# Moving the table products of a two-layer expert kernel, splitting its weight chunks later, and giving its last steps an order of their own

## The reference

```python
# layer 0, weights of the sequence's expert: Wi 256x1024, Wo 1024x256
h = gelu(x @ Wi[e] + bi[e]);  r = h @ Wo[e] + bo[e] + x
x = layernorm(r, eps=1e-12) * gamma[e] + beta[e]
# layer 1: down 256->64, an expert matrix 64x64, up 64->256
a = gelu(x @ down_W.T + down_b)
o = a @ expert_W[d].T + expert_b[d] + domain_emb[d]
x = layernorm(o @ up_W.T + up_b + x, eps=1e-5) * ln_gamma + ln_beta
```

## Time and profile before

| | us |
|---|---|
| median of 3 runs | 488.36 (488.33 to 488.38) |
| profiled execution | 488.29, of which the span from first to last instruction is 486.5 |
| PE busy | 458.1 (94% of the span) |
| ACT busy | 362.3 (74%) |
| DVE busy | 341.8 (70%) |
| POOL busy | 343.7 (71%) |
| mean granted TensorE clock | 0.980 of full speed |
| chain that ended last | PE 89%, DVE 3%, issue 2%, POOL 2%, ACT 2% |

### The profile page before, as it was taken

How to read it: one execution, slowest core, us unless ns; L and a number is a source line. 1 busy time by engine, 2 the same in 40 slices (tenths; PEclk the granted TensorE clock), 3 DMA queues, 4 the chain that set the end, 5 groups by cost and what they waited for, 6 DMA issues and landing times.

```text
span 486.5 us, 18826 instructions
## 1 busy us (share of the span) xinstructions
PE 458.1 (94%) x5724; PEld 423.3 (87%) x5725; DVE 341.8 (70%) x910; ACT 362.3 (74%) x1087; POOL 343.7 (71%) x567
## 2 busy tenths in 40 slices
PE   3599999999999999999999999999999999999972
PEld 2388999999999999999999999999999999888861
DVE  7677777777777777777777787777777766665352
ACT  2499777887777877778877788777787777776631
POOL 5043677887778877887778877887778877754565
PEclk9889999999999999999999999999999999999995
DMA  3924334333333343433433333333332222220001
GB/s 105 333 73 106 95 99 104 104 102 92 98 100 95 103 104 87 99 96 102 104 89 95 102 101 98 86 98 101 101 98 65 60 62 61 62 56 25 26 22 34
DMA packets 66806, 44.33 MB, mean 91 GB/s; under 512 B 41537, under 2 KB 58322, under 8 KB 66642
## 3 DMA queue, kind: packets, MB, share of 16 engines
q1 hardware_dynamic: 65744, 43.68, 33.4%
q10 hardware_dynamic: 1026, 0.21, 0.2%
HBM read 35.47 MB, written 8.39 MB: 90 GB/s over the span
## 4 chain that ended last, share of the span: by engine, by line
PE 89%; DVE 3%; issue 2%; POOL 2%; ACT 2%; DMA 0%; POOLq 0%; DVEq 0%
PE p_o L1019 12%; PE p_o L1017 12%; PE p_o L1018 12%; PE p_h L1006 12%; PE p_h L1008 11%; PE p_h L1007 11%; PE p_d L1029 7%; PE p_u L1043 6%; PE p_t L1051 3%; PE p_u L1039 2%; PE p_o L1117 1%; PE p_h L947 1%; DVE W L810 1%; ACT h L639 0%; ACT ctab L591 0%
## 5 line engine op out<-in xcount | busy, mean ns | idle before, releaser
L1006 PE MATMUL p_h<-x_hi,W 128*128 128x128 f16 (+1 forms) x1088 | 183.5, 217 | 3.3 <-issue 3.3
L1007 PE MATMUL p_h<-x_lo,W 128*128 128x128 f16 (+1 forms) x1088 | 183.3, 217 | 0.0
L1008 PE MATMUL p_h<-x_hi,W 128*128 128x128 f16 (+1 forms) x1088 | 183.3, 217 | 0.0
L639 ACT ACTIVATE h<-p_h,bi_tile 128x128 f32<-128x128 f32 (+1 forms) x544 | 149.0, 359 | 0.0
L1018 PE MATMUL p_o<-W,h_hi 128*128 x512 | 139.6, 273 | 0.0
L1017 PE MATMUL p_o<-W,h_hi 128*128 x512 | 139.6, 273 | 0.0
L1019 PE MATMUL p_o<-W,h_lo 128*128 x512 | 139.5, 273 | 0.0
L1006 PEld LDWEIGHTS p_h<-x_hi,W 128*128 x1088 | 105.7, 98 | 9.3 <-issue 8.0
L1007 PEld LDWEIGHTS p_h<-x_lo,W 128*128 x1088 | 105.7, 98 | 1.9
L1008 PEld LDWEIGHTS p_h<-x_hi,W 128*128 x1088 | 105.6, 98 | 0.0
L539 POOL TENSOR_TENSOR rs<-mv,neg_half 128x1 f32<-128x1 f32 x64 | 55.1, 861 | 69.7 <-DVE mv L882 69.7
(11 more groups left out here) (167 smaller groups left out, 825.5 us busy)
## 6 DMA issues: line engine op xcount, KB each, us to landing
stage<-in_w SPq DMA_DIRECT2D x56, 256.0 KB, 2.7
x_nat<-in_x SPq DMA_DIRECT2D x128, 64.0 KB, 2.1
out<-y SPq DMA_DIRECT2D x128, 64.0 KB, 2.0
x_T<-in_xT SPq DMA_DIRECT2D x126, 64.0 KB, 2.2
W<-in_w SPq DMA_DIRECT2D x8, 256.0 KB, 4.8
g_t<-in_gamma SPq DMA_DIRECT2D x1, 1024.0 KB, 7.0
W<-in_expert_W SPq DMA_DIRECT2D x2, 128.0 KB, 3.0
upT<-in_up_W SPq DMA_DIRECT2D x2, 64.0 KB, 2.6
```

What stands on the lines that cost most here:

```text
L639: ins = nc.scalar.activation(h[:, c, mine], p_h[parity][:, c, mine], ACT.Gelu, bias=bi_tile[:, parity, n, c:c + 1], scale=1.0 / (XS * WS))
L1006: mm(out, hi, x_hi[:, parity, k, mine], start=(k == 0), stop=False)
L1007: mm(out, hi, x_lo[:, parity, k, mine], start=False, stop=False)
L1008: ins = mm(out, lo, x_hi[:, parity, k, mine], start=False, stop=(k == KD - 1))
```

## The change

Six things change.

- **Tables.** All four rounds move behind the first products, one in each of the steps 0 to 3 (`rounds`). Rounds 0 and 1 use `p_t` and `p_d`, rounds 2 and 3 `p_u` and `p_d` (`table_banks`). The matmuls for `u_s` now write `p_h1`. Round r waits for `c_copied` = 2r, `down` of step 3 for 6, `up` of step 4 for 8, round 3 for `a1_done`.
- **Chunks.** Steps 0 to 3 split one chunk each, steps 4 and 5 two each, later steps one as before.
- **First loads.** SP issues four of the first expert's chunks, then x of tile 1, then the other four.
- **Drain.** In steps 64 to 68 DVE has an order of its own, PE transposes behind the second products and not between them, and for tiles 60 to 63 gamma and beta are applied by DVE (`late_gamma`, `late_out`, semaphores `yl_done`, `y_late`), not by POOL.
- **Places.** The two further numbers of a mixed tile stand in the same row of `idx`, which is six wide now; steps 60 to 64 load six numbers at once.
- **Buffers.** The second half of the turned expert matrices lies in `ew[0]`, not in `yg`.

```diff
         def chunks(i, weights):
-            if isinstance(i, int) and i < EARLY:
-                return [(2 * i + q, (2 * i + q, 1, 2 * i + q)) for q in range(2)]
+            if isinstance(i, int) and i < LEAD - EARLY:
+                js = [i] if i < 4 else [2 * i - 4, 2 * i - 3]
+                return [(j, (j, 1, j % SLOTS_W)) for j in js]
             return [(i + EARLY, weights)] if weights else []
...
+        def rounds(i):
+            return [i] if isinstance(i, int) and i < 4 else []
+        def table_banks(r):
+            return [(p_t if r < 2 else p_u)[:, :], p_d[:, :]]
+        def drain(i):
+            return isinstance(i, int) and i >= TILES
+        def late(j):
+            return isinstance(j, int) and TILES - 4 <= j < TILES
...
-            for m in FIRST_ORDER:
-                sp.dma_start(first_stage[m], t["w"][bass.ds((expert + m) * P, P), :]).then_inc(first_in[m], 16)
+            load_first(FIRST_ORDER[:4])
             sp.wait_ge(idx_ready, SRC_READY)
             load_turned(indices(sp, IDX_SP + 6, 2, B - 1), 1, 1)
+            load_first(FIRST_ORDER[4:])
...
 ACT, before the steps
-            copy_round(0, both)
             for n, m in enumerate(FIRST_ORDER):
                 if n == 2:
                     high_x(0, 0)
+                if n == 4:
+                    act.wait_ge(u_summed, 1)
+                    nc.scalar.copy(u_s[:, :], ph_flat[1][:, 0:D]).then_inc(u_ready, 1)
                 act.wait_ge(first_in[m], 16)
                 high(m, 0, first_stage[m]).then_inc(w_first_hi, 1)
-            copy_round(1, both)
...
 ACT and DVE, in a step (low_round the same)
-                if isinstance(i, int) and i < 2:
-                    copy_round(2 + i, [p_t[:, :], p_d[:, :]])
+                for r in rounds(i):
+                    copy_round(r, table_banks(r))
...
 DVE, in the drain
+                def late_gamma():
+                    dve.wait_ge(mv2_done, i - 3)
+                    dve.wait_ge(y_out[parity], loads(i - 6, parity, 2))
+                    v.scalar_tensor_tensor(y[:, parity, :], yg[:, parity, :], mv[:, 1, 0:1], lng[:, :],
+                                           ALU.subtract, ALU.mult).then_inc(yl_done, 1)
+                def late_out():
+                    dve.wait_ge(rs2_done, i - 3)
+                    dve.wait_ge(yl_done, i - 3 - (TILES - 4))
+                    v.scalar_tensor_tensor(y[:, parity, :], y[:, parity, :], rs[:, 1:2], lnb[:, :],
+                                           ALU.mult, ALU.add).then_inc(y_late, 1)
...
 PE
-            c_tables(0, both)
-            pe.wait_ge(c_copied, 2)
-            c_tables(1, both)
...
-                def places(tile, place_reg):
-                    return indices(pe, IDX_MIX + 2 * (tile - PURE), 2, PLACE_TOP) if mixed(tile) else [place_reg]
-                here, there = places(i, here), places(i - 1, there)
+                    for r, top in zip(indices(pe, 6 * i + IDX_PE, 6 if two_places else 4, DOMAIN_TOP),
...
-                if isinstance(i, int) and i == 0:
-                    pe.wait_ge(u_ready, 1)
-                    pe.wait_ge(idx_ready, TILE_READY)
-                    c_tables(2, [p_t[:, :], p_d[:, :]])
-                if isinstance(i, int) and i == 1:
-                    pe.wait_ge(c_copied, 6)
-                    c_tables(3, [p_t[:, :], p_d[:, :]])
+                for r in rounds(i):
+                    if r == 0:
+                        pe.wait_ge(idx_ready, ALL_READY)
+                    else:
+                        pe.wait_ge(c_copied, 2 * r)
+                    if r == 3:
+                        pe.wait_ge(a1_done, 1)
+                    c_tables(r, table_banks(r))
...
-                    if j == TR_AT and exists(i - 2):
+                    if j == TR_AT and exists(i - 2) and not drain(i):
                         transpose()
...
+                if drain(i) and exists(i - 2):
+                    transpose()
```

More of the change, by code:

```diff
@@ L126, in build @@
         ew = [early(0, E1 // 2, A), early(1, E1 // 2, A)]
-        wt = [early(2, 8, A), yg[:, :, :].rearrange("p a (b c) -> p (a b) c", c=A)]
+        wt = [early(2, 8, A), ew[0]]
         embb = early(3, 4, GROUP)
@@ L385, in _, with load_first @@
             expert = first_chunk(0)
-            for m in FIRST_ORDER:
-                sp.dma_start(first_stage[m], t["w"][bass.ds((expert + m) * P, P), :]).then_inc(first_in[m], 16)
+            def load_first(ms):
+                for m in ms:
+                    sp.dma_start(first_stage[m], t["w"][bass.ds((expert + m) * P, P), :]).then_inc(first_in[m], 16)
+            load_first(FIRST_ORDER[:4])
             sp.wait_ge(idx_ready, SRC_READY)
             load_turned(indices(sp, IDX_SP + 6, 2, B - 1), 1, 1)
+            load_first(FIRST_ORDER[4:])
             expert = [first_chunk(1)]
@@ L504, in step @@
                 e_third, e_before, _, _, e_next = indices(pool, i + (IDX_EXP - 3), 5, E0 - 1)
-                if exists(i - 5):
+                if exists(i - 5) and not late(i - 5):
                     last = y[:, 1 - parity, :]
@@ L790, in _ @@
             for n in range(2):
[L791 to L795, removed]
+                for q in range(2):
+                    v.tensor_copy(pe_idx[:, n:TILES + n, 4 * q + 1 - n], by_tile[:, 1, :, q]).then_inc(sort_step, 1)
+            v.tensor_copy(idx[:, IDX_MIX_EXP:IDX_LEN], p_d[0:1, SLOTS + 2 * PURE:2 * SLOTS]).then_inc(sort_step, 1)
+            n_sort[0] += 7
             dve.wait_ge(sort_step, n_sort[0])
@@ L900, in step @@
                                     ALU.subtract, ALU.mult).then_inc(z2_done, 1)
+                def late_gamma():
[8 more added lines that the diff above has]
+                                           ALU.mult, ALU.add).then_inc(y_late, 1)
+                if drain(i):
+                    if exists(i - 1):
+                        split_h(i - 1, 1 - parity, 1)
+                    if exists(i - 2):
+                        residual_1()
+                        aggr_1()
+                    if exists(i - 4):
+                        residual_2()
+                        stats_2()
+                        aggr_2()
+                    if exists(i - 2):
+                        normal_1()
+                    if exists(i - 4):
+                        late_gamma()
+                    if exists(i - 3):
+                        low_a()
+                    if exists(i - 4):
+                        late_out()
+                    return
+                if exists(i - 2):
+                    residual_1()
+                if exists(i - 4):
+                    residual_2()
+                if exists(i - 2):
+                    aggr_1()
+                if exists(i - 4):
+                    stats_2()
+                if exists(i - 3):
+                    low_a()
+                if exists(i - 4):
+                    aggr_2()
+                if exists(i - 1):
+                    split_h(i - 1, 1 - parity, 1)
+                if exists(i - 2):
+                    normal_1()
+                if exists(i + 1):
+                    low_x(i + 1, 1 - parity)
+                if exists(i - 4):
+                    normal_2()
                 for j, (m, place_n, slot_n) in chunks(i, weights):
@@ L1055, in up_weights @@
                     return ctab_flat[:, bass.ds(domains[n] + part * D, D)]
-                there, here, *domains = [
+                two_places = mixed(i) or mixed(i - 1)
+                there, here, *rest_of = [
                     nc.s_assert_within(r, 0, top, skip_runtime_bounds_check_because="the sorting clips every index")
-                    for r, top in zip(indices(pe, 4 * i + IDX_PE, 4, DOMAIN_TOP), 2 * [PLACE_TOP] + 2 * [DOMAIN_TOP])]
-                def places(tile, place_reg):
-                    return indices(pe, IDX_MIX + 2 * (tile - PURE), 2, PLACE_TOP) if mixed(tile) else [place_reg]
-                here, there = places(i, here), places(i - 1, there)
+                    for r, top in zip(indices(pe, 6 * i + IDX_PE, 6 if two_places else 4, DOMAIN_TOP),
+                                      2 * [PLACE_TOP] + 2 * [DOMAIN_TOP] + 2 * [PLACE_TOP])]
+                domains = rest_of[0:2]
+                here = [here] + (rest_of[3:4] if mixed(i) else [])
+                there = [there] + (rest_of[2:3] if mixed(i - 1) else [])
                 if exists(i):
@@ L1093, in step @@
                         down()
-                if isinstance(i, int) and i == 0:
-                    pe.wait_ge(u_ready, 1)
-                    pe.wait_ge(idx_ready, TILE_READY)
-                    c_tables(2, [p_t[:, :], p_d[:, :]])
-                if isinstance(i, int) and i == 1:
-                    pe.wait_ge(c_copied, 6)
-                    c_tables(3, [p_t[:, :], p_d[:, :]])
-                if isinstance(i, int) and i == 2:
-                    pe.wait_ge(c_copied, 8)
+                for r in rounds(i):
+                    if r == 0:
+                        pe.wait_ge(idx_ready, ALL_READY)
```

(7 more changed lines are left out.)

56 lines of the change are left out of this document (25 added, 31 removed).

## The result

The changed kernel took 490.0 us (median of 18 runs, 488.57 to 492.16), the kernel before beside it 488.32 (487.81 to 488.79). The ratio is 1.0033, with a 95% interval of 1.0025 to 1.0041: a third of a per cent slower, where 480.3 was forecast. Its runs also spread over 3.6 us, where those of before spread over 1.0.

The account below looks back on a forecast made before the run. PE was taken as the bound in the steady steps, leaving only its start, mixed-tile gaps and drain to win: 3.3 + 2.4 + 2.4 = 8.1 from 488.29, forecast 480.3 us (median), range 477.0 to 484.0.

Parts of the forecast that it names:

- the term for the early steps: Start to step 4: first product and PE's early steps come sooner, bias product of step 4 at 48.9; gain 3.3 us.
- Slower than before: Rival, early steps: the loop through SP sets the pace, needing turns of 9 us or more; 489.5 or above; chance 0.02.
- the 7.7 of a step with a round: Early steps: a step lengthened by a table round takes 7.7 us; the SP loop of 6.2 stays under it.
- I take 0.5: Steps 1 to 4: 0.5 us allowed for waits from ACT's lateness and x arriving a step later; bounds 0 and 2.0.
- a sign that the prediction named for being wrong: Idle above 1 us at `down` of step 3 or `up` of step 4 would show the forecast wrong.
- the 47.5 to 51 that it named for being right: Bias product of step 4 starting between 47.5 and 51 us would show the forecast right.
- The rest of the start: Start: x lands at 16.1, first product at 17.0 to 17.1, tile 0 takes 4.9 us, wait before round 1 is 0.4.
- The mixed tiles: Steps 60 to 63: one load of six numbers replaces separate loads, cutting PE's gaps from 3.3 us; gain 2.4.
- What a wider load costs PE no row shows: Mixed tiles: PE's wider-load cost held not visible, so taken from SP's queue: 0.13 us for two more numbers.
- the 0.065 a number: Mixed tiles: each further number in a load costs 0.065 us, from SP's gaps of 0.71 and 0.97.
- loads cost by the number: Rival, mixed tiles: a load of six costs as much as four and two; gain 1.3, 481.4 to 482.7; chance 0.12.
- The drain: Steps 64 to the end: earlier second products and z1, POOL's late work gone; 0.22 + 0.2 + 1.9, taken as 2.4 us.

Follow-up runs that it names:

- splits ahead of a1s: Changed kernel with DVE in steps 0 to 5 splitting the step's chunks ahead of a1s, h_lo, z and x_lo: 481.72 us, ratio 0.9869.
- cured kernel: Changed kernel with SP in steps 0 to 5 issuing the x loads before the stage chunk load, splits still late: 479.31 us, ratio 0.9822.
- the cure in the late steps only: Changed kernel with x loaded before the stage chunk only in SP's steps 3 to 5: 482.88 us, ratio 0.9881.
- the late schedule alone: Kernel before with only the new chunk schedule, and PE not waiting for w_lo in steps 2 to 5: 498.04 us, ratio 1.0202.
- late splits with SP's order cured: Kernel before with the new chunk schedule and x loaded before the stage chunk in SP's steps 0 to 5: 488.19 us, ratio 0.9994.

## Why the prediction was wrong

- **The step that failed** is the term for the early steps, "a gain of 3.3", and in it the loop of the rival "Slower than before": "0.33 + 0.54 + 0.6 + 4.2 and some 0.5, or 6.2 us, under the 7.7 of a step". The loop was named and its members on SP and the DMA sized well (from chunk load to x landed 4.2 forecast, 47.83 to 52.7 or 4.9 measured). Left out was what stands ahead of the split in DVE's program: a1s, which waits for ACT's a and a1s, then the mean and variance, h_lo, z, x_lo and y, and in step 4 the high part of a second chunk on ACT. The chunk loads of SP give 9.0 and 9.9 us a turn where a1s exists. The splits ahead of a1s (481.7) show that it was this for most of the loss, and x before the chunk (479.3) that SP's order closed the loop. The other side of the comparison was off too: "the 7.7 of a step with a round" is a full step and a round, and the early steps, in which `up`, `down` or a transposition is still missing, take 6.6 and 7.3 with one (cured kernel), so a turn of 7.6 already costs. The chance of 0.02 rested on a sum over the instructions with data between them, and not over the engines' queues.
- **"I take 0.5"** for the waits of steps 1 to 4 was the same mistake in small. The first three turns cost 3.6, by the cure in the late steps only. There were waits at the table rounds and at `down` (1.15 and 1.94 in the trace), but ACT had got x late there; with x early the table rounds have one wait of 0.8 and `down` none. The 1.94 at `down` of step 3 is a sign that the prediction named for being wrong, and the bias product of step 4 at 53.09 lies outside the 47.5 to 51 that it named for being right.
- **The rest of the start held.** x of tile 0 came at 17.25 and not 16.1, so the first product at 18.18 and not 17.1; the products of tile 0 started at the spacing of half clock for 3.6 us and not 4.3, so that they took 4.5 and not 4.9; the wait ahead of round 1 was 0.8 and not 0.4. Cured, the bias product of step 4 is at 48.68 (48.9 forecast), and the start is worth 2.8 to 3.5 (3.3 forecast).
- **The mixed tiles**: 2.2 timed alone, 2.4 forecast. By the gaps it is 3.0 (from 3.3 to 0.35). "What a wider load costs PE no row shows" was not so: the profile records every register load, and PE's (last section) give two numbers 0.53 us (one load of eight in steps 60 to 64 took 0.67), four 1.00 and six 1.47, or 0.33 for four and 0.83 for six in every second step. SP's two gaps of the earlier trace rows held a load of two (0.49, at 12.7) and one of the cheap loads of six (0.74, at 28.2), so the 0.065 a number was far too low: on PE two more numbers cost 0.47 (1.00 to 1.47) or 0.50 (0.33 to 0.83). What made up for it is that with rows of six every second load starts at a cheap place, which the prediction did not have. That the forecast came near is luck. The rival "loads cost by the number", whose 1.3 is a third load in three steps at the 0.43 by which the gaps of the earlier trace rows differ (0.45 and 0.88), is out as it was sized: its 0.45 should have stayed in each of four steps, and 0, 0.17 and 0.18 were left. But its price for the load itself is right in steps 60, 62 and 64, where six numbers take 1.47 and four and two took 1.00 + 0.53.
- **The drain**: 1.9 alone, 2.4 forecast. `late_gamma` ran beside POOL's power and y ended 1.3 behind the last statistics (483.20 to 484.54) where 3.3 stood before. Together with the places it gave 5.6, where 4.8 was forecast.
- The sum of everything but the loop, 8.1, came out at 9.2 (488.5 to 479.3 on one chip). The forecast was wrong by one term, and by its sign; that the other terms came near was in part luck, as for the wide loads.

## What to carry over

When a change moves work between steps, write down each loop that crosses engines (a load that waits for a split that waits for the load) and sum it along the engines' queues: at every engine, all that stands ahead of the awaited instruction counts with its own waits, not only the instruction. Where such a loop is longer than the step of the bounding engine (here 9.9 us a turn against 6.67), it sets the time, however idle each engine in it looks. Take that step from the same stretch: the first steps here were shorter than a full one. In a DMA queue, a load that somebody needs soon goes ahead of one that first has to wait; here swapping the two in six steps turned 490.0 into 479.3.

## What the runs showed of the hardware that I had not expected

- **A register load costs by its numbers and, it seems, by their place.** These are PE's loads of four numbers in the kernel before, then its first five in the mixed tiles (four, two, four, two, two numbers), each with count and duration in ns, shortest/median/longest:

```profile
L274 PEldq TENSOR_LOAD <-idx x54: 997/1002/1017, 60.2 to 415.4; - x54
```

```profile
L274 PEldq TENSOR_LOAD <-idx x5: 529/534/1002, 422.1 to 431.3; - x5
```

  And in the changed kernel, the loads of four, then the five loads of six:

```profile
L276 PEldq TENSOR_LOAD <-idx x52: 328/670/1014, 80.6 to 422.7; - x52
```

```profile
L276 PEldq TENSOR_LOAD <-idx x5: 823/1472/1474, 429.4 to 465.7; - x5
```

  One by one, the loads of four take 0.33 and 1.00 by turns, and those of six 1.47 in steps 60, 62 and 64 and 0.83 in 61 and 63. The cheap ones are those whose first number has a place in `idx` that divides by four (IDX_PE is 414, and a row is six wide now); with rows of four numbers every load of four lay two off and took 1.00. SP's loads of six take 0.74 and 1.28 by the same rule. The kernel with the places alone differs from the one before in its loads of four only by their place, and they too take 0.33 and 1.00 by turns. That it is the division by four is read from this pattern; no run tried other places. About 1.00 is hidden in a step with one load, which has no gap. So in step 60 the merged load saves little more than the 0.2 between two loads (gap 0.45 to 0.17), in step 62 also two numbers, eight having become six (0.99 to 0.18), and in steps 61 and 63 the cheap place as well (0.88 and 1.03 to nothing). The 0.98 of "issue" in the drain is also a load of four: it starts at 473.13, with the transposition, and takes 1.00.
- **The granted clock of a window can be wrong ahead of its first recorded change.** In the changed kernel the window shows full clock where the products still start 0.10 to 0.11 apart, as they do in the kernel before from 24.57 to 26.0, where its windows show 0.50:

```profile
20.00:21.00 1.00, 1.00 (x12) 1.00 (x11) 1.00 (x3) 0.80 (x3) 0.00 (x0) 1.00 1.12 305
```

```profile
20.08 0.31 PE L1079 MATMUL p_h<-x_hi,W 128*128 128x128 f16 x1
20.18 0.31 PE L1080 MATMUL p_h<-x_lo,W 128*128 128x128 f16 x1
```

  Their spacing halves (0.05 to 0.06) only at 21.8. So in this trace the spacing of the products tells the clock at the start, and the means (0.980 before, 0.988 after) say nothing of a faster PE.
- **The runs of the kernels with the closed loop spread.** Those of the changed kernel spread over 3.6 us (18 runs) and those of the late schedule alone over 3.1 (5), those of before over 1.0 (18). In the loop each turn holds a landing, which took 2.2 to 3.6 us in this stretch. That this is the reason is not shown: with the loop open the runs still spread over 2.0 (x before the chunk, 5 runs) and 1.9 (late splits with SP's order cured, 12 runs).
